# Feature attention stage: one score block copied by ScalarE, k's features clamped by GpSimd and drained by ScalarE

## Chip, cores and metric

One core of one Trainium2 chip. The metric is the device time of one execution in microseconds (us). The engines are PE (TensorE), DVE (VectorE), ACT (ScalarE), POOL (GpSimd) and SP (queue of transfers).

## What is computed

The network has four stages, each followed by a LayerNorm: a linear attention, a mixture of experts, a causal attention with softmax features, and a deep stage of six layers that takes most of the time. The input has 16 sequences of 256 positions and width 128, all in fp32. The change is in the third stage alone:

```python
def _feature_map(t, K):
    f = jnp.einsum('hdf,bhld->bhlf', K, t)
    feats = jnp.concatenate([jax.nn.softmax(f, axis=-1), jax.nn.softmax(-f, axis=-1)], axis=-1)
    return jnp.maximum(feats, EPS)              # EPS = 1e-12
qf = _feature_map(q, Kq); kf = _feature_map(k, Kk)
kv = jnp.cumsum(kf[:, :, :, None, :] * v[..., None], axis=2)
o = jnp.einsum('bhlf,bhldf->bhld', qf, kv)
z = jnp.einsum('bhlf,bhlf->bhl', qf, jnp.cumsum(kf, axis=2)) + EPS
o = o / z[..., None]                            # then heads side by side, @ Wo
```

There are 16 heads of 64. The cumulative sum is computed as causal attention: scores of kf and qf, those above the diagonal set to zero, times v.

## The kernel before

All five engines run programs of their own, ordered by hand and joined by counting semaphores. In the feature stage the unit of the order is the *step*: the function `heads` of each engine loops over h = 0 to 15, one head of sequence n for each step, and puts between the heads the preparation of sequences n+1 and n+2, at steps given by tables of constants. Every engine works its queue strictly in the written order. Sequences 1 to 12 run in a loop that holds two of them; the rest are written out.

**Preparation of a sequence.** It has four *units*: unit 0 is q and unit 1 is k of the first 128 positions, units 2 and 3 are q and k of the second. PE projects in *slots* (L791), each into the one bank `gen`; ACT copies each out (L921, L927) before the next can start. For each unit DVE takes the largest and smallest value of each head (L986, L994), POOL subtracts (L1104, L1107), ACT takes the exponential (L910, 128x2048), DVE sums and takes the reciprocal (L1002, L1004), POOL multiplies (L1116, `scale`) and signals `featured`. PE then turns the unit to feature-major in four slots (L804), in steps 0 to 3 for unit 0, 4 to 7 for unit 1, 8 to 11 for unit 2, 12 to 15 for unit 3. The slots alternate between two banks, `trn`. DVE drains each with a maximum against 1e-12 into `qT` or `kT` (L1012, `keep_features`). Sums and reciprocals stand in steps 13 (the unit 0 of the next sequence), 2, 6 and 10. Projections stand in steps 1 to 13.

**A head.** PE computes three 128x128 blocks of scores into one bank (L817, L818): keys 0 to 127 against all 256 queries, and keys 128 to 255 against queries 128 to 255. The first and third lie on the diagonal; the middle one has all its scores valid. DVE multiplies all three with a table of ones and zeros, `tri` (L1029, `mask`). PE multiplies by V (L829 to L831, `mix`), one step later than the scores. After every second head, in the odd steps, DVE divides by z (L1036, L1039, L1044, `drain_pair`). The outputs are turned (L843), drained by ACT (L939) and multiplied by Wo (L851) in steps 3 and 4; DVE adds them to X (L1051).

Order of PE in step h: scores(h), projection, turning slot h, mix(h-1), then output work. Order of DVE in step h: drain_pair (odd h), maxima, minima or sums where due, mask(h), keep_features of slot h, the addition in step 5. Order of ACT in step h: copy of the projection, exponential (steps 11, 0, 4, 8), drain of the turned output. POOL repeats: subtract unit 0, scale unit 3 of the sequence before, subtract 1, scale 0, copy x, subtract 2, scale 1, subtract 3, scale 2.

Before the first head, PE's slots of sequence 0 and the first of sequence 1 run alone; this is called the lead-in here.

Of the kernel before, what the change touches and what calls it, by code (L numbers as in the profile page):

```python
# [12 lines left out]
ALU = mybir.AluOpType  # L13
# [694 lines left out]
def feature_stage(nc, X, c, weights):  # L708
    with ExitStack() as ctx:
        def sb(name, shape, dt=F32):  # L710
            return ctx.enter_context(nc.sbuf_tensor(name, shape, dt))
# [24 lines left out]
        zr = sb("g_zr", [P, 2, 4])  # L736
        on = sb("g_on", [P, 2, H, HD])
        oT = sb("g_oT", [P, PAIRS, SEQ])
        sco = [psum("g_sco0"), psum("g_sco1")]
        tur = psum("g_tur")  # L740
        wop = tur
# [15 lines left out]
        summed = sem("g_summed")  # L757
        recips = sem("g_recips")
        featured = sem("g_featured")
        scored = sem("g_scored")  # L760
        masked = sem("g_masked")
        mixed = sem("g_mixed")
        z_kept = sem("g_z_kept")
        z_recip = sem("g_z_recip")
# [14 lines left out]
        def _(pe):  # L779
# [15 lines left out]
            def turn_features(n, step, first=False):  # L795
                for slot in [i for i, at_step in enumerate(F_TURN_STEPS) if at_step == step]:
                    unit, a = divmod(slot, 4)

                    if not (first and slot < 2):
                        pe.wait_ge(turn_kept, count(n * F_TURN + slot - 1))  # L800
                    pe.wait_ge(featured, count(n * 4 + unit + 1))
                    for i in range(4):

                        t = pe.transpose(trn[slot % 2][:, i * P:(i + 1) * P],  # L804
                                         ex[:, unit % 2, 4 * a + i].rearrange("p s f -> p (s f)"), c["ident"][:])
                    t.then_inc(turn_full, 1)

            def scores(n, par, h, first):
                N = n * H + h
                if h == 0:  # L810

                    pe.wait_ge(turn_kept, count(n * F_TURN + F_TURN))
                    pe.wait_ge(proj_drained, count(n * F_PROJ + F_PROJ))
                if not (first and h < 2):
                    pe.wait_ge(masked, count(N - 1))
                s = sco[h % 2]
                pe.matmul(s[:, 0:SEQ], kT[:, par, h, 0:P], qT[:, par, h], start=True, stop=True)  # L817
                pe.matmul(s[:, SEQ:SEQ + P], kT[:, par, h, P:SEQ], qT[:, par, h, P:SEQ],  # L818
                          start=True, stop=True).then_inc(scored, 1)

            def mix(n, par, h, first=False):
                N = n * H + h
                pe.wait_ge(masked, count(N + 1))
                if h % 2 == 0 and not (first and h < 4):

                    pe.wait_ge(head_out, count(n * PAIRS + h // 2 - 1))
                a, o = at[:, h % 2], (h % 2) * 130
                bank = acc[h // 2 % 2]
                pe.matmul(bank[:, o:o + 65], a[:, 0:P], V[:, par, 0, h], start=True, stop=True)  # L829
                pe.matmul(bank[:, o + 65:o + 130], a[:, P:SEQ], V[:, par, 0, h], start=True, stop=False)  # L830
                pe.matmul(bank[:, o + 65:o + 130], a[:, SEQ:SEQ + P], V[:, par, 1, h],  # L831
                          start=False, stop=True).then_inc(mixed, 1)
# [68 lines left out]
        @block.scalar  # L901
        def _(act):
            def exps(n, unit, first):

                j = n * 4 + unit
                act.wait_ge(shift_done, count(2 * j + 2))
                if not (first and unit < 2):

                    act.wait_ge(turn_full, count(4 * (j - 1)))
                act.activation(ex[:, unit % 2].rearrange("p h s f -> p (h s f)"),  # L910
                               shifted[:, unit % 2].rearrange("p h s f -> p (h s f)"), ACT.Exp).then_inc(exped, 1)

            def project(n, par, step, first=False):
                for slot in [i for i, at_step in enumerate(F_PROJ_STEPS) if at_step == step]:
                    act.wait_ge(proj_full, count(n * F_PROJ + slot + 1))
                    if slot == 0:
                        t = act.activation(xT[:], gen[:, 0:SEQ], ACT.Copy)
                    else:
                        k, part, a = F_PROJ_ORDER[slot - 1]
                        if part == 2:  # L920
                            t = act.activation(V[:, par, k, 8 * a:8 * a + 8, 0:HD],  # L921
                                               gen[:].rearrange("p (h d) -> p h d", d=HD), ACT.Copy)
                        else:
                            if a == 0 and not first:

                                act.wait_ge(shift_done, count(2 * (n * 4 - 4 + 2 * k + part) + 2))
                            t = act.activation(raw[:, k, part, a * 512:a * 512 + 512], gen[:], ACT.Copy)  # L927
                    t.then_inc(proj_drained, 1)

            def exponentials(n, step, first=False):  # L930
                if step in F_EXP_STEPS:
                    exps(n, F_EXP_STEPS.index(step), first)

            def drain_out(n, q):
                act.wait_ge(o_turned, count(4 * n + q + 1))
                if q == 0:

                    act.wait_ge(projected, count(n))
                act.activation(oT[:, 2 * q:2 * q + 2], tur[:].rearrange("p (r t) -> p r t", t=SEQ),  # L939
                               ACT.Copy).then_inc(oT_ready, 1)  # L940

            def heads(n, par, first=False, ahead=2):
                for h in range(H):
                    if ahead >= 1:
                        project(n + 1, 1 - par, h)
                    if ahead >= 2:
                        project(n + 2, par, h - H)
                    if ahead >= 1:
                        exponentials(n + 1, h)
                    if ahead >= 2:  # L950
                        exponentials(n + 2, h - H)
                    if h in F_OUT_TURN_STEPS:
                        drain_out(n, F_OUT_TURN_STEPS.index(h))
                    if h + H in F_OUT_TURN_STEPS and not first:
                        drain_out(n - 1, F_OUT_TURN_STEPS.index(h + H))

            act.preload_act_table(ACT.Exp)
            act.wait_ge(ready, 1)
            act.wait_ge(ones_set, count(1))
            for step in range(F_FIRST, H):  # L960
                project(0, 0, step, True)
                project(1, 1, step - H)
                exponentials(0, step, True)
                exponentials(1, step - H)
            heads(0, 0, first=True)
            with act.Fori(0, NSEQ // 2 - 2) as i:
                heads(2 * i + 1, 1)
                heads(2 * i + 2, 0)
            heads(NSEQ - 3, 1)
            heads(NSEQ - 2, 0, ahead=1)  # L970
            heads(NSEQ - 1, 1, ahead=0)
            for q, step in enumerate(F_OUT_TURN_STEPS):
                if step >= H:
                    drain_out(NSEQ - 1, q)
# [3 lines left out]
        def _(dve):  # L978
# [27 lines left out]
            def keep_features(n, par, step):  # L1006

                for slot in [i for i, at_step in enumerate(F_TURN_STEPS) if at_step == step]:
                    unit, a = divmod(slot, 4)
                    k, part = divmod(unit, 2)  # L1010
                    dve.wait_ge(turn_full, count(n * F_TURN + slot + 1))
                    dve.tensor_scalar((qT, kT)[part][:, par, 4 * a:4 * a + 4, k * P:(k + 1) * P],  # L1012
                                      trn[slot % 2][:].rearrange("p (h t) -> p h t", t=P), 1e-12, None,
                                      ALU.max).then_inc(turn_kept, 1)

# [8 lines left out]
            def mask(n, h, first):  # L1024
                N = n * H + h
                dve.wait_ge(scored, count(N + 1))
                if not (first and h < 2):
                    dve.wait_ge(mixed, count(N - 1))
                dve.tensor_tensor(at[:, h % 2], sco[h % 2][:, 0:3 * P], tri[:], ALU.mult).then_inc(masked, 1)  # L1029

            def drain_pair(n, r, first=False):
                Q = n * PAIRS + r
# [59 lines left out]
        def _(pool):  # L1092
# [18 lines left out]
            def scale(n, unit):  # L1111
# [1 line left out]
                part = unit % 2  # L1113
                pool.wait_ge(recips, count(j + 1))
                e = ex[:, part]
                pool.tensor_tensor(e, e, er[:, part][:, :, :, None].to_broadcast([P, H, 2, HD]), ALU.mult)\  # L1116
                    .then_inc(featured, 1)

            def stage(n):

# [15 lines left out]
                scale(n, 2)  # L1136

            pool.wait_ge(ready, 1)
            stage(0)
            project(0, first=True)  # L1140
            with pool.Fori(1, NSEQ - 1) as n:
# [1167 lines left out]
```

## Time and profile before

| | |
|---|---|
| median of 3 runs | 4956.29 us (4952.42 to 4957.85) |
| profiled execution, its time | 4950.25 us |
| its span, first to last instruction | 4948.6 us |
| PE busy | 4317.4 us (87%) |
| DVE busy | 3975.7 us (80%) |
| ACT busy | 3045.9 us (62%) |
| POOL busy | 2752.6 us (56%) |
| feature stage | from 493 us to 1284 us of the span |

Busy times are sums over the whole program. The feature stage is about a sixth of the span, and what bounds it has to be read inside it: from the busy times of one sequence, and from what each engine waits for.

### The profile page before, as it was taken

To read this page: it belongs to the slowest core of one execution; us is meant where nothing else is said; L and a number is where in the kernel's file an instruction comes from. 1 tells how busy PE (TensorE), PEld (TensorE's weight loads), DVE (VectorE), ACT (ScalarE), POOL (GpSimd) and SP (SyncE) were. 2 spreads that over 40 slices of the span, in tenths; PEclk is the share of its full clock that TensorE was granted. 3 is DMA by queue.
4 is the path that set the end of the run, shared out by engine and by line. 5 is a ranking of instruction groups with operands and counts; after the bars stand their busy time and mean duration, and the time that the engine had idled before them with its cause. 6 is when DMAs were issued, how large, how long until landed. Compare 5 with 4: busy or idle time off the path is not lost. (4 is left out here: it accounts for less than half of the span.)

```text
span 4948.6 us, 174542 instructions
## 1 busy us (share of the span) xinstructions
PE 4317.4 (87%) x70208; PEld 3409.7 (69%) x70208; DVE 3975.7 (80%) x6281; ACT 3045.9 (62%) x5515; POOL 2752.6 (56%) x1392
## 2 busy tenths in 40 slices
PE   5797899999589899899998998989989989999985
PEld 4565577777467777777777776777777777777774
DVE  5334799998688889888898888988889888998883
ACT  3365333333257777776777777777777767777763
POOL 0222666666266566665666556655666556666561
PEclk9799899999789999999999999999999999999997
DMA  1233000000132233322333224233233232332232
GB/s 48 93 122 119 1 1 0 0 0 1 35 70 58 65 70 82 83 61 57 85 78 74 64 57 99 64 68 71 57 88 77 64 69 66 81 83 60 60 68 55
DMA packets 239161, 303.67 MB, mean 61 GB/s; under 512 B 93940, under 2 KB 129272, under 8 KB 237944
## 3 DMA queue, kind: packets, MB, share of 16 engines
q1 hardware_dynamic: 223192, 247.08, 21.9%
q0 software_dynamic: 15264, 46.14, 2.9%
q8 instruction: 571, 9.36, 0.8%
q14 instruction: 134, 1.10, 0.1%
HBM read 50.37 MB, written 28.84 MB: 16 GB/s over the span
## 5 line engine op out<-in xcount | busy, mean ns | idle before, releaser
L2100 POOL TENSOR_TENSOR raw<-raw,rs 128x1024 f32<-128x1024 f32 x384 | 792.9, 2065 | 1089.7 <-DVE rs L1937 627.8
L2092 POOL TENSOR_TENSOR spare<-raw,table 128x1024 f32<-128x1024 f32 x384 | 914.9, 2393 | 261.7 <-DVE raw L1916 250.8
L1909 DVE TENSOR_TENSOR raw<-raw,table 128x1024 f32<-128x1024 f32 x384 | 732.2, 1907 | 42.4 <-POOL spare L2092 40.4
L1781 ACT ACTIVATE raw<-shared 128x512 f32<-128x512 f32 x768 | 463.5, 603 | 333.9 <-PE shared L1559 310.9
L1557 PE MATMUL shared<-wqkv_lo,xT_hi 128*128 128x512 f32 x1152 | 567.5, 493 | 33.0 <-DVE xT_lo L1946 25.8
L1903 DVE TENSOR_REDUCE ss<-spare 128x16 f32<-128x1024 f32 x384 | 466.1, 1214 | 155.1 <-ACT spare L1786 154.2
L1916 DVE TENSOR_TENSOR raw<-raw,spare 128x1024 f32<-128x1024 f32 x384 | 550.8, 1434 | 13.2
L1612 PE MATMUL trn<-ident,raw 128*128 128x128 f32 x3072 | 484.0, 280 | 13.5 <-POOL raw L2100 4.0
L1558 PE MATMUL shared<-wqkv_hi,xT_lo 128*128 128x512 f32 x1152 | 474.1, 412 | 0.0
L1559 PE MATMUL shared<-wqkv_hi,xT_hi 128*128 128x512 f32 x1152 | 472.2, 410 | 0.0
L1786 ACT ACTIVATE spare<-shared 128x512 f32<-128x512 f32 x768 | 462.3, 602 | 1.9 <-DVE ss L1903 1.9
L1612 PEld LDWEIGHTS trn<-ident,raw 128*128 128x128 f32 x3072 | 351.2, 141 | 142.8 <-issue 49.9
L1665 PE MATMUL acc<-prT,Vw 64*64 64x32 f32 x24576 | 439.0, 221 | 0.1
L1819 ACT ACTIVATE prT<-trn 128x512 f32<-128x512 f32 x384 | 232.2, 605 | 319.6 <-PE trn L1647 317.6
L1665 PEld LDWEIGHTS acc<-prT,Vw 64*64 64x64 f32 x24576 | 396.1, 135 | 23.4 <-issue 0.4
L2115 POOL TENSOR_TENSOR E<-E,rden 128x1024 f32<-128x1024 f32 x192 | 366.4, 1908 | 40.9 <-DVE rden L1982 33.8
L1632 PE MATMUL sco<-kT,qT 64*32 64x64 f32 (+1 forms) x24576 | 378.7, 232 | 11.8 <-issue 11.5
L1647 PE MATMUL trn<-ident,E 128*128 128x128 f32 x1536 | 276.6, 310 | 128.6 <-POOL E L2115 125.8
L1632 PEld LDWEIGHTS sco<-kT,qT 64*32 64x32 f32 x24576 | 255.3, 113 | 187.6 <-issue 183.2
L1681 PE MATMUL shared<-wo,oT 128*128 128x128 f32 x3072 | 376.6, 276 | 2.3 <-ACT oT L1828 1.3
L1681 PEld LDWEIGHTS shared<-wo,oT 128*128 128x128 f32 x3072 | 363.8, 193 | 8.8 <-ACT spare L1786 1.5
L1647 PEld LDWEIGHTS trn<-ident,E 128*128 128x128 f32 x1536 | 214.1, 161 | 192.9 <-issue 148.3
(203 smaller groups left out, 9723.9 us busy)
## 6 DMA issues: line engine op xcount, KB each, us to landing
Vw<-V SPq DMA_DIRECT2D x1344, 128.0 KB
xs<-X SPq DMA_DIRECT2D x144, 128.0 KB, 2.1
Vw<-V SPq DMA_DIRECT2D x192, 64.0 KB
e_plain<-in_L_ffn_W SPq DMA_DIRECT2D x16, 704.0 KB, 4.7
split_hi<-e_high POOLq DMA_DIRECT2D x16, 704.0 KB, 5.9
split_lo<-e_low POOLq DMA_DIRECT2D x16, 704.0 KB, 7.1
wqkv_hi<-split_hi POOLq DMA_DIRECT2D x30, 256.0 KB, 3.1
wqkv_lo<-split_lo POOLq DMA_DIRECT2D x30, 256.0 KB, 3.2
```

What stands on the lines that cost most here:

```text
L1557: pe.matmul(to, a_hi, b_lo, start=True, stop=False)
L1558: pe.matmul(to, a_lo, b_hi, start=False, stop=False)
L1559: return pe.matmul(to, a_hi, b_hi, start=False, stop=True)
L1612: t = pe.transpose(trn[:, r * P:(r + 1) * P], raw[:, par, k, part, at:at + P], c["ident"][:])
L1632: t = pe.matmul(sco[g * WIN:g * WIN + WIN, hp, at:at + back + WIN], qT[lo:lo + 64, r, at_q:at_q + WIN], kT[lo:lo + 64, r, at_q - back:at_q ...
L1647: t = pe.transpose(trn[:, i * P:(i + 1) * P], e[:, 4 * jj + i], c["ident"][:])
L1665: t = pe.matmul(acc[hp][64 * jp:64 * jp + 64, at:at + WIN], Vw[lo:lo + 64, par, k, g, (4 * o + j) * HD:(4 * o + j + 1) * HD], prT[lo:lo + ...
L1681: t = pe.matmul(to[:, k * P:(k + 1) * P], oT[:, r, k * P:(k + 1) * P], wo[:, r], start=(r == 0), stop=(r == PAIRS - 1))
L1909: dve.tensor_tensor(x, x, table[:, part, 0, k][:, None, :].to_broadcast([P, H, HD]), ALU.mult).then_inc(cos_part, 1)
L1916: dve.tensor_tensor(x, x, t2[:, part], ALU.add).then_inc(summed, 1)
L2092: pool.tensor_tensor(dst, src, by[:, None].to_broadcast([P, H, 2, 32]), ALU.mult).then_inc(sin_part, 1)
L2100: pool.tensor_tensor(x, x, rs[:, at:at + H][:, :, None].to_broadcast([P, H, HD]), ALU.mult).then_inc(rotated, 1)
```

## The change

For each head ACT copies the middle block of the scores (`cross`), at the head of its step, and DVE multiplies the two diagonal blocks alone, with one 128x128 table broadcast. ACT's copy waits for DVE's mask of the same head. For the units of k (1 and 3) POOL takes the maximum against 1e-12 itself, after `scale`, with a one-column operation on a tile of its own, `dot`, between the two; `featured` is signalled after the maximum. ACT then copies the turned slots of k out (`keep_k`), at the end of its step, and DVE's `keep_features` does q's slots only. PE waits for both of `masked` and `crossed`, and for `turn_kept` or `k_kept`.

```diff
@@ PE, turn_features
-                        pe.wait_ge(turn_kept, count(n * F_TURN + slot - 1))
+                        last = (slot - 2) % F_TURN
+                        freed = 8 * n - 8 * (slot < 2) + 4 * (last // 8) + last % 4 + 1
+                        pe.wait_ge(k_kept if last // 4 % 2 else turn_kept, count(freed))
@@ PE, scores
-                    pe.wait_ge(turn_kept, count(n * F_TURN + F_TURN))
+                    pe.wait_ge(turn_kept, count(8 * n + 8))
+                    pe.wait_ge(k_kept, count(8 * n + 8))
                     pe.wait_ge(proj_drained, count(n * F_PROJ + F_PROJ))
                 if not (first and h < 2):
                     pe.wait_ge(masked, count(N - 1))
+                    pe.wait_ge(crossed, count(N - 1))
@@ PE, mix
                 pe.wait_ge(masked, count(N + 1))
+                pe.wait_ge(crossed, count(N + 1))
@@ ACT
+            def keep_k(n, par, step):
+                for slot in [i for i, at_step in enumerate(F_TURN_STEPS) if at_step == step]:
+                    unit, a = divmod(slot, 4)
+                    k, part = divmod(unit, 2)
+                    if part == 0:
+                        continue
+                    act.wait_ge(turn_full, count(n * F_TURN + slot + 1))
+                    act.activation(kT[:, par, 4 * a:4 * a + 4, k * P:(k + 1) * P],
+                                   trn[slot % 2][:].rearrange("p (h t) -> p h t", t=P), ACT.Copy).then_inc(k_kept, 1)
+            def cross(n, h, first):
+                N = n * H + h
+                act.wait_ge(masked, count(N + 1))
+                if not (first and h < 2):
+                    act.wait_ge(mixed, count(N - 1))
+                act.activation(at[:, h % 2, P:SEQ], sco[h % 2][:, P:SEQ], ACT.Copy).then_inc(crossed, 1)
@@ ACT, heads
                 for h in range(H):
+                    cross(n, h, first)
                     if ahead >= 1:
                         project(n + 1, 1 - par, h)
...
+                    if ahead >= 1:
+                        keep_k(n + 1, 1 - par, h)
+                    if ahead >= 2:
+                        keep_k(n + 2, par, h - H)
                     if h in F_OUT_TURN_STEPS:
@@ DVE, keep_features
+                    if part == 1:
+                        continue
                     dve.wait_ge(turn_full, count(n * F_TURN + slot + 1))
-                    dve.tensor_scalar((qT, kT)[part][:, par, 4 * a:4 * a + 4, k * P:(k + 1) * P],
+                    dve.tensor_scalar(qT[:, par, 4 * a:4 * a + 4, k * P:(k + 1) * P],
@@ DVE, mask
-                dve.tensor_tensor(at[:, h % 2], sco[h % 2][:, 0:3 * P], tri[:], ALU.mult).then_inc(masked, 1)
+                own, to = (x.rearrange("p (c t) -> p c t", t=P)[:, 0:3:2] for x in (sco[h % 2][:, 0:3 * P], at[:, h % 2]))
+                dve.tensor_tensor(to, own, tri[:, None, 0:P].to_broadcast([P, 2, P]), ALU.mult).then_inc(masked, 1)
@@ POOL, scale
-                pool.tensor_tensor(e, e, er[:, part][:, :, :, None].to_broadcast([P, H, 2, HD]), ALU.mult)\
-                    .then_inc(featured, 1)
+                i = pool.tensor_tensor(e, e, er[:, part][:, :, :, None].to_broadcast([P, H, 2, HD]), ALU.mult)
+                if part == 1:
+                    i.then_inc(scaled, 1)
+                    pool.wait_ge(scaled, count(2 * n + unit // 2 + 1))
+                    pool.tensor_tensor(dot[:], dot[:], dot[:], ALU.mult)
+                    i = pool.tensor_scalar(e, e, 1e-12, None, ALU.max)
+                i.then_inc(featured, 1)
```

The rest of the diff declares `dot` and the three semaphores, sets `dot` to zero once, and calls `keep_k` in the lead-in too.

## Rows read from the trace of the kernel before

**Rows 1.** POOL's timeline: the copies of x of two sequences (start us, duration, instruction).

```profile
837.93 0.40 POOL L1121 COPY g_xs<-X 128x256 f32 x1
...
884.33 0.40 POOL L1121 COPY g_xs<-X 128x256 f32 x1
```

**Rows 2.** Busy time of each engine in 46 us of the steady loop.

```profile
836.00:882.00 46.00, 44.08 (x297) 36.40 (x296) 42.14 (x73) 17.13 (x21) 29.36 (x14) 1.00 0.00 0
```

**Rows 3.** PE's waits, 500 to 1300 us: total us, times, longest.

```profile
PE g_acc L829 <- DVE g_at L1029: 18.1, 15, 1.3
...
PE g_sco L817 <- DVE g_kT L1012: 8.8, 15, 0.8
```

**Rows 4.** Groups of instructions, whole program: busy us, mean ns, idle before.

```profile
L1116 POOL TENSOR_TENSOR g_ex<-g_ex,g_es 128x2048 f32<-128x2048 f32 x64 | 231.8, 3621 | 26.7 <-DVE g_es L1004 26.7
...
L462 POOL COPY e_xs<-X 128x512 f32 x14 | 8.6, 617 | 19.2 <-PE e_xb L512 19.2
...
L1121 POOL COPY g_xs<-X 128x256 f32 x14 | 5.6, 396 | 0.0
```

**Rows 5.** The same view: rows of DVE and ACT.

```profile
L1029 DVE TENSOR_TENSOR g_at<-g_sco,g_tri 128x384 f32<-128x384 f32 x256 | 137.5, 537 | 35.7 <-PE g_sco L818 35.1
...
L1044 DVE TENSOR_TENSOR g_on<-g_acc,g_zr 128x256 f32<-128x256 f32 x128 | 54.3, 424 | 7.1
```

```profile
L604 ACT ACTIVATE e_ggT<-e_tb 128x128 f32<-128x128 f32 x288 | 77.7, 272 | 4.9 <-PE e_ob L562 4.5
```

**Rows 6.** Timeline, steps 1 to 4 of one sequence.

```profile
839.36 0.16 DVE L1036 TENSOR_SCALAR g_zs<-g_acc 128x4 f32<-128x4 f32 x1
...
841.23 0.55 DVE L1029 TENSOR_TENSOR g_at<-g_sco,g_tri 128x384 f32<-128x384 f32 x1
...
843.54 0.60 ACT L921 ACTIVATE g_V<-g_gen 128x512 f32<-128x512 f32 x1 [2.02 <-PE g_gen L791]
...
844.87 0.49 DVE L1029 TENSOR_TENSOR g_at<-g_sco,g_tri 128x384 f32<-128x384 f32 x1
...
845.11 3.62 POOL L1116 TENSOR_TENSOR g_ex<-g_ex,g_es 128x2048 f32<-128x2048 f32 x1
...
845.50 1.02 PE L791 MATMUL g_gen<-g_wf,g_xT 128*128 128x512 f32 x2
...
850.77 0.60 PE L804 MATMUL g_trn<-ident,g_ex 128*128 128x128 f32 x4
```

**Rows 7.** Timeline, steps 10 to 12 of the same sequence.

```profile
869.56 0.49 DVE L1029 TENSOR_TENSOR g_at<-g_sco,g_tri 128x384 f32<-128x384 f32 x1
...
869.81 3.62 POOL L1116 TENSOR_TENSOR g_ex<-g_ex,g_es 128x2048 f32<-128x2048 f32 x1
...
870.19 1.02 PE L791 MATMUL g_gen<-g_wf,g_xT 128*128 128x512 f32 x2
...
873.67 0.60 PE L804 MATMUL g_trn<-ident,g_ex 128*128 128x128 f32 x4
```

**Rows 8.** Timeline, step 12 to the next sequence's step 0.

```profile
874.31 0.69 DVE L1012 TENSOR_SCALAR g_kT<-g_trn 128x512 f32<-128x512 f32 x1 [0.27 <-PE g_trn L804]
...
874.50 0.39 PE L831 MATMUL g_acc<-g_V,g_at 128*128 128x65 f32 x2
...
874.93 0.16 DVE L1036 TENSOR_SCALAR g_zs<-g_acc 128x4 f32<-128x4 f32 x1
...
879.38 0.49 DVE L1029 TENSOR_TENSOR g_at<-g_sco,g_tri 128x384 f32<-128x384 f32 x1
...
879.93 0.44 PE L829 MATMUL g_acc<-g_V,g_at 128*128 128x65 f32 x2 [1.27 <-DVE g_at L1029]
...
882.65 0.68 DVE L1012 TENSOR_SCALAR g_kT<-g_trn 128x512 f32<-128x512 f32 x1
...
883.57 0.67 PE L817 MATMUL g_sco<-g_qT,g_kT 128*128 128x256 f32 x2 [0.56 <-DVE g_kT L1012]
```

**Rows 9.** PE's queue: one of its semaphore waits (ns).

```profile
L826 PEldq EVENT_SEMAPHORE  x54: 51/51/51, 574.6 to 1274.3; - x54
```

More of the change, by code:

```diff
@@ L738, in feature_stage @@
         oT = sb("g_oT", [P, PAIRS, SEQ])
+        dot = sb("g_dot", [P, 1])
         sco = [psum("g_sco0"), psum("g_sco1")]
@@ L759, in feature_stage @@
         featured = sem("g_featured")
+        scaled = sem("g_scaled")
+        k_kept = sem("g_k_kept")
         scored = sem("g_scored")
         masked = sem("g_masked")
+        crossed = sem("g_crossed")
         mixed = sem("g_mixed")
@@ L964, in _ @@
                 exponentials(1, step - H)
+                keep_k(0, 0, step)
             heads(0, 0, first=True)
@@ L1138, in _ @@
             pool.wait_ge(ready, 1)
+            pool.memset(dot[:], 0.0)
             stage(0)
```

## Prediction

> **What bounds the stage now.** I read the page first: the feature stage is a sixth of the span, so I went on inside it. POOL's timeline gives the period: from one copy of x to the next are 46.40 us for each sequence [rows 1]. The busy times of that stretch say what fills it [rows 2]: PE 44.1 of 46 us, DVE 42.1, ACT 17.1, POOL 29.4. PE is the bound and DVE is close behind. PE keeps all its work, so only its idle time can be won. The view of PE's waits has two that come back in each of 15 sequences [rows 3]: a mix that waits for a mask, 18.1 us in all, and the first scores that wait for the last keep of k, 8.8 us. Their sum, 27 us, is about all that relieving DVE can bring. Last I read the timeline of one sequence, to see what each late instruction follows from [rows 6 to 8].
>
> The mix that waits is mix(13), in step 14 [rows 8]. Its mask starts at 879.38, and the work before it on DVE begins at 874.93, with the division that needs mix(11), which ended on PE at 874.50 + 0.39 = 874.89. So that wait is a chain of latencies from PE through DVE (division, minima, sums, mask) and back, not a backlog. The keep of k that stands before the division and that the change takes away ended at 875.00, no later than mix(11) plus 0.1: removing it gives almost nothing there.
>
> The second thing to see is that turning slot 12 is already just in time. POOL scales unit 3 from 869.81 to 873.43, and PE's turning matmul starts at 873.67 [rows 7], 0.24 later. POOL has no slack at this place, though it idles a third of the period.
>
> **The change by its parts, for each sequence.**
>
> *DVE's mask.* 537 ns for 384 columns; the 256-column operation on a PSUM input and a broadcast one takes 424 [rows 5]. So 0.12 less, 16 times: 1.9 us off DVE. *DVE's keeps of k*: 8 of 0.68 [rows 8], 5.4 us off. DVE falls from 42.1 to about 35. Neither is on PE's path except through the chains below.
>
> *ACT.* The copy of 128 columns of PSUM takes 0.27 [rows 5], the keep 0.60 like a projection's copy [rows 6]. 16 x 0.27 + 8 x 0.60 = 9.1 us: ACT goes to 26. Its load is no problem; its order is. The copy `cross` stands at the head of ACT's step and waits for the mask; behind it are queued the copy of the projection, on which PE's next projection waits (one bank), the exponential and the keep of k.
>
> *POOL.* The maximum over 128x2048 does not occur in the trace. Bounds: like the copies, one input read, 396 ns for 256 columns and 617 for 512, thus 0.863 ns a column, 0.396 + 1792 x 0.000863 = 1.94 us; or like the two-input multiply, 3.62 us [rows 4]. It reads one tensor, so I take 1.94. The one-column operation costs the copies' fixed part, 0.396 - 256 x 0.000863 = 0.18, and the wait for the scale's own end some 0.05 (the gap from a mask's end, 879.87, to PE's mix, 879.93 [rows 8]). Together 2.2 us later for `featured`, twice a sequence. POOL goes to 34 us: still not full.
>
> The measured slope of 0.863 ns a column has a rule beside it: the Trainium skill, GPSIMD Engine Reference, section on elementwise cycle accounting, puts a body of up to two operations per element at 1.03 cycles at 1.2 GHz, 0.86 ns, and the trace agrees. The same section gives 1.8 cycles as the best case of a tight loop; by it the maximum would be an estimated 3.1 us, between my two bounds.
>
> *PE.* One more wait in each scores and each mix, 32 a sequence, of 51 ns in its queue [rows 9]. They stand behind matmuls of 0.4 to 1.0 us that are still running, so I take nothing; wholly exposed they would be 1.6 us a sequence, 24 us in all.
>
> **The chains on PE's path.**
>
> *Step 2 to 3.* DVE's chain from the division at 839.36 over mask(1) at 841.23 to mask(2) at 844.87 [rows 6] becomes 0.12 shorter, by the one shorter mask. Mask(2) then ends at 844.75 + 0.37 = 845.12; cross: 845.17 to 845.44; the projection's copy, 0.60: 846.04, and 0.05 to PE: 846.09. PE has wanted the bank at 845.50; ACT had freed it at 843.54 + 0.60 = 844.14. A new stall of 0.6.
>
> *Step 4.* POOL's scale of unit 1, 845.11 + 3.62, + 2.2 + 0.24 = 851.2. PE wants slot 4 at 850.77, now 0.6 later, 851.4 [rows 6]. No stall, by 0.2.
>
> *Step 10 to 12.* Mask(10): 869.44 + 0.37 = 869.81; with cross and copy 870.78, PE had wanted 870.19 [rows 7]: 0.6. But this is swallowed by the next: slot 12 is ready at 873.43 + 2.2 + 0.24 = 875.87 in place of 873.67. POOL's start at 869.81 follows its own subtraction and the minima of step 9, which no part of the change makes earlier. The stall is 2.2.
>
> *Step 13 to 0.* Everything from mix(11) moves by 2.2: mask(13) to 881.58, end 881.95, cross to 882.27, mix(13) at 882.3 instead of 879.93: +2.4. Behind that cross ACT has in its queue the projection's copy, keep, cross(14), keep, cross(15), keep: 4 x 0.60 + 2 x 0.27 = 2.9, ending at 885.2. The first scores follow 0.24 later, at 885.4, where they started at 883.57 [rows 8]: +1.9. The old wait on DVE's last keep (0.56) is so given back in part.
>
> Sum: 0.6 + 1.9 = 2.5 us a sequence. Features are prepared for sequences 1 to 15 inside the heads, 15 times: 37 us. In the lead-in POOL's extra 2.2 us come twice, against DVE queues that are shorter there; I take 0 to 2 us less, 1. By the profiled execution: 4950.3 + 36 = 4986; its time was 6 below the median of the runs, so **4992 us** on the scale of that median.
>
> **Rivals.**
>
> *1. POOL's maximum costs as much as a two-input operation*, 3.62. Then slot 12 comes 1.68 later still, and slot 4 stalls too, by 1.68 - 0.2 = 1.5: 2.5 + 3.2 = 5.7 a sequence, 85 us: **5040**. For it: all of POOL's large operations in this stage cost that. Against: those read two tensors. The rule of 1.8 cycles in the page above lies on this side.
>
> *2. Faster.* If slot 12 is not delayed, DVE's relief can take away both waits of [rows 3], 27 us: **4929**. It needs POOL's clamp to end within the present slack of slot 12, about zero, thus the sums of unit 3 some 2.2 us earlier; it decides from there. For it: DVE loses 7 of 42 us, and sums are its work. Against: the scale starts when POOL's subtraction ends, and the mask of step 13 hangs on mix(11).
>
> *3. No difference.* ACT's held-up copies cost nothing (ACT overlaps them, or the masks come earlier), and relief on DVE removes the wait of mix(13), 1.2 a sequence, and of the first scores, 0.6. Then 2.2 - 1.8 = 0.4, 6 us: **4962**. For it: two waits of DVE do stand on PE's path. Against: the mask of step 13 starts by a chain.
>
> *4. Only POOL's delay counts*, and nothing waits behind ACT's masks and copies: 2.2 at slot 12, less 0.12 for the shorter mask of step 13 and 0.56 for the first scores' wait, which goes [rows 8]: 1.5 a sequence, 23 us: **4979**. For it: ACT is busy a third of the period. Against: its order, above.
>
> **Numbers.** My forecast 0.55, rival 1 0.17, rival 2 0.06, rival 3 0.08, rival 4 0.14. A measurement of this kernel can tell about 0.2%, 10 us, from no change. Faster 0.06, same 0.08, slower 0.86. The likeliest case's own range is 4982 to 5005. The range of 8 in 10 runs from below rival 4 to most of rival 1, with part of PE's exposed waits: 4968 to 5032.
>
> **What would show it.** The period between copies of x: 48.9 instead of 46.4. POOL's maximum: 1.94, right behind a small operation. The matmul of slot 12 waiting for POOL in every sequence, 2 us; the mix of step 14 still waiting, now for ACT's copy; the projection of step 3 waiting 0.5 for ACT. DVE at 35 us and PE at 44 in each period. Wrong would be: a maximum at 3.6; a mask of step 13 that starts much less than 4.4 after mix(11); or PE's queue shown as what its scores and mixes wait for.

## Result and the profile after

The changed kernel takes **5201.83 us** (median of 4 runs, 5199.6 to 5204.28), beside 4957.07 for the kernel before (median of 4): a ratio of 1.0495, 95% interval 1.0477 to 1.0513. The forecast was 4992 with a range of 4968 to 5032: the sign is right, the size is wrong by a factor of seven (245 us more, where 36 were forecast).

I read the profile after in the order of the prediction. POOL's timeline first: the copies of x of two sequences, and what stands between them (start us, duration, instruction).

```profile
855.92 0.40 POOL L1162 COPY g_xs<-X 128x256 f32 x1
...
863.10 3.62 POOL L1152 TENSOR_TENSOR g_ex<-g_ex,g_es 128x2048 f32<-128x2048 f32 x1
866.80 0.19 POOL L1156 TENSOR_TENSOR g_dot<-g_dot 128x1 f32<-128x1 f32 x1
866.95 5.36 POOL L1157 TENSOR_SCALAR g_ex<-g_ex 128x2048 f32<-128x2048 f32 x1
...
914.08 0.40 POOL L1162 COPY g_xs<-X 128x256 f32 x1
```

The period is 914.08 - 855.92 = 58.16 us, against 46.40 in [rows 1]. The maximum takes **5.36 us**; the prediction took 1.94, and its upper bound was the multiply's 3.62, which is unchanged [rows 4]. The small operation ahead of it takes 0.19, as forecast (0.18).

The busy times of that period, then of a part of it without long waits, then of two stretches that stand at PE's two long waits (length, PE, PEld, DVE, ACT, POOL, then the granted clock as a share of full speed; the first row answers to [rows 2]):

```profile
855.92:914.08 58.16, 49.99 (x299) 40.39 (x298) 36.05 (x65) 24.19 (x45) 40.76 (x18) 0.91 0.00 0
856.00:870.00 14.00, 13.34 (x84) 10.42 (x84) 10.52 (x19) 5.72 (x11) 10.86 (x6) 1.00 0.00 0
873.40:876.60 3.20, 3.20 (x17) 3.20 (x17) 1.89 (x4) 0.25 (x1) 0.69 (x1) 0.50 0.00 0
901.00:907.40 6.40, 5.05 (x16) 3.86 (x17) 2.65 (x5) 0.60 (x1) 1.89 (x2) 0.50 0.00 0
```

DVE is at 36.05 as forecast (35) and ACT at 24.19 (26): the work was moved as the change says. POOL is at 40.8, not 34. PE has about as many matmuls as in a period of before (299 and 301), but is busy 50 us with them and not 44.6, and the clock was granted at 0.91, not 1.00. What is new is in the last two rows: PE was granted 0.50, the lower of its two levels, 1.2 GHz in place of 2.4. The first of these stretches goes from about 873.3 to 876.7, 3.4 us, and begins 1 us after the wait ended; the second from about 900.8 to 907.6, 6.8 us, and begins while PE still waits. PE's timeline, steps 4 and 12, shows the waits:

```profile
872.36 0.66 PE L810 MATMUL g_trn<-ident,g_ex 128*128 128x128 f32 x4 [2.89 <-POOL g_ex L1157]
...
873.62 3.48 PE L860 MATMUL g_tur<-g_wo,g_oT 128*128 128x128 f32 x16
876.94 0.60 PE L825 MATMUL g_sco<-g_qT,g_kT 128*128 128x256 f32 x2
...
902.35 1.12 PE L810 MATMUL g_trn<-ident,g_ex 128*128 128x128 f32 x4 [4.51 <-POOL g_ex L1157]
...
904.44 1.16 PE L825 MATMUL g_sco<-g_qT,g_kT 128*128 128x256 f32 x2
...
905.82 1.83 PE L795 MATMUL g_gen<-g_wf,g_xT 128*128 128x512 f32 x2
```

PE waits 2.89 us for the maximum at slot 4 and 4.51 at slot 12. The projection's two matmuls behind the second take 1.83, where they took 1.02 [rows 7]; the 16 of the output product behind the first take 3.48, where they took 2.00:

```profile
847.41 2.00 PE L851 MATMUL g_tur<-g_wo,g_oT 128*128 128x128 f32 x16
```

The groups of 700 to 1300 us, and PE's wait in 560 to 1400 (total, times, longest), which answer to [rows 3 to 5]:

```profile
L1157 POOL TENSOR_SCALAR g_ex<-g_ex 128x2048 f32<-128x2048 f32 x20 | 107.1, 5355 | 0.0
L1065 DVE TENSOR_TENSOR g_at<-g_sco,g_tri 128x256 f32<-128x256 f32 x166 | 66.6, 404 | 47.0 <-PE g_sco L826 46.9
L946 ACT ACTIVATE g_kT<-g_trn 128x512 f32<-128x512 f32 x83 | 49.9, 601 | 56.7 <-PE g_trn L810 56.7
L959 ACT ACTIVATE g_at<-g_sco 128x128 f32<-128x128 f32 x165 | 46.0, 279 | 286.7 <-DVE g_at L1065 286.3
...
PE g_trn L810 <- POOL g_ex L1157: 116.4, 30, 7.7
```

All prices but POOL's came as forecast: the mask 0.40 (0.42), the keep on ACT 0.60, the block's copy 0.28 (0.27).

**A second part that the prediction doesn't have.** The stage ends with the last addition to X. Its row before and its row after:

```profile
1284.08 0.42 DVE L1051 TENSOR_TENSOR X<-X,g_tur 128x256 f32<-128x256 f32 x1 [5.28 <-PE g_tur L851]
```

```profile
1468.28 0.42 DVE L1087 TENSOR_TENSOR X<-X,g_tur 128x256 f32<-128x256 f32 x1 [6.90 <-PE g_tur L860]
```

Up to there the changed kernel has lost 184 us: 11.8 in each of 15 periods, 177, and 7 besides, of which 6 stand in the lead-in (its third copy of x starts at 567.29 in place of 561.35). What follows, the *deep part* from here on, is untouched by the diff, and yet takes 5198.0 - 1468.3 = 3729.7 in place of 4948.6 - 1284.1 = 3664.5: **65 us more**. The view of waits names a line: the score matmuls of the deep stage's loop wait for "issue", that is for nothing that the profile shows. Before, then after:

```profile
PE sco L1632 <- issue: 11.5, 27, 2.2
```

```profile
PE sco L1674 <- issue: 66.9, 31, 3.7
```

PE's timeline at the start of one pass of that loop, before and after:

```profile
2091.05 0.60 PE L1622 MATMUL sco<-mask,identb 128*128 128x512 bf16 x2 [3.57 <-issue]
2091.59 1.04 PE L1632 MATMUL sco<-kT,qT 64*32 64x32 f32 x64
...
2095.30 0.46 PE L1632 MATMUL sco<-kT,qT 64*32 64x64 f32 x12 [0.73 <-issue]
```

```profile
2285.26 0.60 PE L1664 MATMUL sco<-mask,identb 128*128 128x512 bf16 x2 [3.88 <-issue]
2285.79 0.34 PE L1674 MATMUL sco<-kT,qT 64*32 64x32 f32 x17
2289.84 0.96 PE L1674 MATMUL sco<-kT,qT 64*32 64x64 f32 x47 [3.70 <-issue]
```

Both kernels stop for 3.6 to 3.9 us at the loop's first instruction. The second stop comes after 92 matmuls and lasts 0.73 before; after, it comes behind 19 matmuls and lasts 3.70. The same loop, the same instructions, another place in the program.

### The profile page after: what moved, and what is told of

Its sections match the earlier page's. It is cut to its first block and busy times, and to the rows that moved or that the text cites. A ratio compares the mean times of both kernels' runs of the same rounds, so it can differ in the third digit from the quotient of the medians.

```text
span 5198.0 us, 175762 instructions
## 1 busy us (share of the span) xinstructions
PE 4380.4 (84%) x70208; PEld 3456.7 (67%) x70208; DVE 3885.6 (75%) x6153; ACT 3163.1 (61%) x5899; POOL 2929.0 (56%) x1457
## 5 line engine op out<-in xcount | busy, mean ns | idle before, releaser
L1951 DVE TENSOR_TENSOR raw<-raw,table 128x1024 f32<-128x1024 f32 x384 | 746.0, 1943 | 50.2 <-POOL spare L2134 48.3
```

What stands on the lines that cost most here:

```text
L1951: dve.tensor_tensor(x, x, table[:, part, 0, k][:, None, :].to_broadcast([P, H, HD]), ALU.mult).then_inc(cos_part, 1)
```

## The experiments

**Where the code stands: before_pad, after_pad.** Counting PE's instructions in the two programs, the deep loop starts at 6143 before and at 6294 after: the change adds 151, waits for the most part. (A matmul counts as two, its weight load and itself.) In both the second stop lies at instruction 6343 (about 200, and about 49, behind the loop's start). So I moved the loop alone: 151 increments of an unused semaphore on PE ahead of the deep stage of the kernel before, and 49 in the changed kernel.

```diff
+        padded = sem("padded")
...
+            for _ in range(151):
+                pe.sem_inc(padded, 1)
             pe.wait_ge(filled, count(FILLED))
```

> The kernel before, with 151 one-time semaphore increments on PE's queue ahead of the deep stage: it puts PE's code of the deep stage where the changed kernel has it, and changes nothing else. Theory: 65 of the 245 us lie in the deep stage and come from where PE's code stands; PE's second stop behind each loop start (2.3 to 3.7 us where the kernel before shows 0.7) appears here too: 4957 + 65 + 8 for the increments = about 5025 to 5030. Rival: the deep stage is slower for something that the feature stage leaves behind: then 4957 to 4965.

> The changed kernel, with 49 one-time semaphore increments on PE's queue ahead of the deep stage, 200 instructions after the kernel before in place of 151. Theory of the code's place, with pages of 256 instructions: the deep loop starts just at a page's end or start, PE's second stop goes, and the deep stage falls to about 3665 us or less, in all 5202 - 65 = 5137. Rival: no effect, 5202 to 5205.

before_pad: 5024.53 us, ratio 1.0149 (1.0132 to 1.0166) with an unchanged feature stage (period 46.40, last addition at 1284.1). Its deep part is 3746.8 us, 82 longer, of which the increments are 12.6 (PE's idle time ahead of the stage is 45.9 in place of 33.3): 70 from the place alone. after_pad: 5136.69, 65 us less than the changed kernel, deep part 3663.9, as before. The waits of before_pad, then of after_pad:

```profile
PE sco L1633 <- issue: 67.5, 28, 4.0
```

```profile
PE sco L1675 <- issue: 2.4, 5, 1.0
```

That settles the 65 us: the place of the loop makes them, and moving it by 49 instructions takes them back.

**One whole page: before_pad256.** The same edit with 256 increments, to see whether the effect repeats.

> The kernel before with 256 increments on PE's queue ahead of the deep stage. If what counts is the place of the loop's start within pages of 256 instructions, the deep stage is as in the kernel before, though the code stands farther than with 151: about 4951 + 10 to 20 for the increments, and PE's second stop of 2 to 4 us is absent. Rival, that the slowdown grows with the distance or has another period: 5010 or more.

4983.24 us, ratio 1.0055 (1.0036 to 1.0073). The deep part is 3699.2; the increments took 28.7 of that (PE idle 62.0 ahead of it in place of 33.3), so 3670 remain, 6 above the kernel before, though more instructions were added than in before_pad:

```profile
PE sco L1633 <- issue: 11.4, 19, 2.6
```

So the kernel before and this one, 256 instructions apart, behave alike, and those moved by 151 and by 200 behave otherwise. That fits a period of 256 instructions; no further distance was run to show that it repeats. The Trainium skill, Runtime: NRT & Kernel Launch, section on instruction fetch mechanics, states that instructions are fetched in blocks of 256, in order, and that a taken branch to a target outside the present window stops the engine for a fetch. These runs agree with it: the first stop of a pass, at the loop's first instruction, takes 3.6 to 3.9 us. The page does not speak of the second stop; that it is the fetch of the next block, and is the longer the sooner PE gets there (3.70 us behind 19 matmuls, 0.73 behind 92), is inferred from these rows.

**The maximum's price: clamp_as_copy, no_clamp, prices.** In the changed kernel, first the maximum replaced by a copy in place (which reads and writes the same bytes, and leaves the clamp of k out), then both of POOL's new operations removed (k's clamp left out too).

```diff
-                    i = pool.tensor_scalar(e, e, 1e-12, None, ALU.max)
+                    i = pool.tensor_copy(e, e)
```

```diff
-                if part == 1:
-                    i.then_inc(scaled, 1)
-                    pool.wait_ge(scaled, count(2 * n + unit // 2 + 1))
-                    pool.tensor_tensor(dot[:], dot[:], dot[:], ALU.mult)
-                    i = pool.tensor_scalar(e, e, 1e-12, None, ALU.max)
```

> The changed kernel with POOL's maximum over k's features replaced by POOL's copy of the same tile onto itself: k's clamp at 1e-12 is left out. The theory of the chains as predicted, with a price of 1.94 for this operation: the period of a sequence 48.9 us (46.4 before, 58.2 after), the feature stage 791 + 36 = 827 us, and with the 65 us of the deep stage 5058 in all. Rival, that ACT's order costs more than was reckoned: the period stays above 51, over 5090.

> The changed kernel without POOL's maximum and its one-column operation: k's clamp at 1e-12 is left out. If all of the feature stage's loss follows from POOL's operation, the period is 46.4 or less; by the chains, ACT's order alone costs 0.6 to 1.2 a sequence: period 47.0 to 47.6, total 4957 + 65 + 9 to 18 = 5031 to 5040. If DVE's relief pays, the period is 44.5 and the total 4993.

clamp_as_copy: 5048.12 us, ratio 1.0193 (1.0175 to 1.0211). The copy takes 1.89, so this is the kernel that the prediction costed. POOL's timeline:

```profile
904.72 0.40 POOL L1162 COPY g_xs<-X 128x256 f32 x1
...
916.63 1.89 POOL L1157 COPY g_ex<-g_ex 128x2048 f32<-128x2048 f32 x1
...
954.54 0.40 POOL L1162 COPY g_xs<-X 128x256 f32 x1
```

The periods are 48.9, as forecast, and in every second sequence up to 955 us 49.8. The longer ones begin with a stretch at the lower clock, here from 902 to 905.5; in the periods from 954.54 on the clock is at 1.00 and none is longer than 48.9:

```profile
902.20:905.40 3.20, 3.20 (x16) 3.11 (x15) 1.66 (x3) 1.29 (x3) 2.92 (x2) 0.50 0.00 0
```

PE's waits in 560 to 1200:

```profile
PE g_acc L838 <- DVE g_at L1065: 20.1, 13, 1.5
PE g_trn L810 <- POOL g_ex L1157: 14.7, 14, 1.3
```

The first row names DVE, but the timeline of one such wait reads otherwise. The two masks are those of heads 13 and 14, back to back; mix(13) needs the first, which ends near 949.95, and ACT's copy behind it, which ends at 950.27. Mix(13) starts 0.14 after that, so it waits for the copy, as predicted; the profile names head 14's mask, which ends in the same moment.

```profile
949.59 0.69 DVE L1065 TENSOR_TENSOR g_at<-g_sco,g_tri 128x256 f32<-128x256 f32 x2
949.99 0.28 ACT L959 ACTIVATE g_at<-g_sco 128x128 f32<-128x128 f32 x1 [4.88 <-DVE g_at L1065]
...
950.41 0.41 PE L838 MATMUL g_acc<-g_V,g_at 128*128 128x65 f32 x2 [1.55 <-DVE g_at L1065]
```

no_clamp: 5028.77, ratio 1.0155 (1.0138 to 1.0173), a period of 47.68 at a clock of 1.00. Both still pay for the deep loop's place (deep parts 3728.6 and 3729.2), since PE's code is that of the changed kernel. Without POOL's clamp the two moves still cost 47.68 - 46.40 = 1.28 us a sequence: relief on DVE gave nothing that ACT's copies did not take back.

prices puts twelve operations one after the other on POOL in the lead-in of the kernel before, each waiting for the one ahead.

```diff
+            tried = [lambda: pool.memset(a, 1.0), lambda: pool.memset(b, 1.0),
+                     lambda: pool.tensor_copy(o, a),
+                     lambda: pool.tensor_scalar(o, a, 1e-12, None, ALU.max),
...
+                     lambda: pool.tensor_tensor(o, a, b, ALU.add),
+                     lambda: pool.tensor_tensor(o, a, b, ALU.mult)]
+            for k, op in enumerate(tried):
+                op().then_inc(probed, 1)
+                pool.wait_ge(probed, k + 2)
```

> The kernel before, with twelve POOL operations one after the other on unused tiles at the start of the feature stage (their results are not used). If the price of 5.36 us belongs to the form tensor_scalar, then maximum, multiply and add by a constant all cost about 5.36 at 128x2048 and grow with the columns at 2.6 ns each (2.7 us at 1024), whether in place or not. If it belongs to the maximum, multiply and add cost 1.9 to 2.0. If it comes of working in place, the one not in place costs 1.9. The copy of 2048 columns: 1.9; tensor_tensor with two full inputs 3.6.

POOL's timeline of it: a copy, a maximum of 2048 columns, the same in place, a maximum of 1024 and 256 columns, a multiply with a constant, maximum and multiply in one, and a sum of two whole tensors. (A sum with a constant took 5.37.)

```profile
495.51 1.89 POOL L1143 COPY g_shifted<-g_ex 128x2048 f32<-128x2048 f32 x1
497.50 5.38 POOL L1144 TENSOR_SCALAR g_shifted<-g_ex 128x2048 f32<-128x2048 f32 x1
502.95 5.36 POOL L1145 TENSOR_SCALAR g_ex<-g_ex 128x2048 f32<-128x2048 f32 x1
508.39 2.77 POOL L1146 TENSOR_SCALAR g_shifted<-g_ex 128x1024 f32<-128x1024 f32 x1
511.24 0.84 POOL L1147 TENSOR_SCALAR g_shifted<-g_ex 128x256 f32<-128x256 f32 x1
512.17 5.37 POOL L1148 TENSOR_SCALAR g_shifted<-g_ex 128x2048 f32<-128x2048 f32 x1
...
523.08 7.09 POOL L1150 TENSOR_SCALAR g_shifted<-g_ex 128x2048 f32<-128x2048 f32 x1
530.25 4.49 POOL L1151 TENSOR_TENSOR g_shifted<-g_ex 128x2048 f32<-128x2048 f32 x1
```

The price belongs to the form of the instruction, one tensor and a constant, and not to the maximum, to writing in place, or to the reads. The program took 5002.82 us in its single execution; only its rows are used.

**One move at a time: cross_only, keep_on_act.** Of cross_only the edit is the changed kernel's `cross` and halved mask, of keep_on_act the lines below. cross_only keeps ACT's copy of the middle block and leaves k's keeps (with their clamp) on DVE; 46 increments put its deep loop 200 instructions behind that of the kernel before, at the place that it has in after_pad (deep part 3668.6, and no second stop but one of 0.9 us). keep_on_act takes the kernel before and gives ACT k's keeps, with 1e-12 added in place of the maximum; masks stay whole on DVE.

```diff
-                    dve.tensor_scalar((qT, kT)[part][:, par, 4 * a:4 * a + 4, k * P:(k + 1) * P],
+                    dve.tensor_scalar(qT[:, par, 4 * a:4 * a + 4, k * P:(k + 1) * P],
...
+                    act.activation(kT[:, par, 4 * a:4 * a + 4, k * P:(k + 1) * P],
+                                   trn[slot % 2][:].rearrange("p (h t) -> p h t", t=P), ACT.Identity,
+                                   bias=dot[:]).then_inc(k_kept, 1)
```

> Of the change only the copy of the middle block by ACT; k's keeps and their clamp stay on DVE, POOL as before; 46 increments put the deep stage's code clear of the bad place. By the chains, ACT's copy of each projection waits for the mask and then for the cross: stalls of 0.5 to 0.6 in steps 3 and 11, 0.2 in steps 12 and 14: period 47.5 to 48.2, total 4951 + 17 to 27 + 5 for the increments = 4973 to 4983. Rival, that DVE's shorter masks pay for it: period 46.4 or less, 4956 at most.

> Of the change only the move of k's keeps to ACT; ACT adds 1e-12 instead of taking the maximum, POOL and the masks are as before. The first scores' wait for DVE's last keep (0.56 a sequence) goes. By that alone: 15 x 0.56 = 8 us faster, 4943. But POOL's scale of unit 0 is ready for turning slot 0 only at 884.38 in the kernel before, 0.8 after the first scores, and hangs on mix(11) through the minima of step 13 and POOL's subtraction: if this chain sets the period, nothing is gained: period 46.4, 4951.

cross_only: 4980.36 us, ratio 1.0048 (1.0031 to 1.0066), periods of 48.4, and 49.3 in every fourth sequence, where again the clock is at 0.50 for about 3.4 us. PE's timeline shows the price as the prediction described it, a projection that waits for the copy queued behind the block's, and a mix that waits for the block's:

```profile
970.69 1.12 PE L795 MATMUL g_gen<-g_wf,g_xT 128*128 128x512 f32 x2 [0.46 <-ACT g_raw L933]
...
992.41 0.41 PE L835 MATMUL g_acc<-g_V,g_at 128*128 128x65 f32 x2 [1.54 <-ACT g_at L956]
```

keep_on_act: 4944.76, ratio 0.9976 (0.9965 to 0.9987), and a period of 46.40, to the hundredth that of before. DVE is at 37.7 in 46 us and not at 42.1. The wait of the first scores [rows 3] is gone, and turning slot 0, right behind them, waits for POOL instead; PE's waits in 560 to 1200:

```profile
PE g_acc L836 <- DVE g_at L1062: 17.9, 14, 1.3
PE g_trn L810 <- POOL g_ex L1149: 7.2, 14, 0.9
```

So two chains end together at the turn of the period. The second is in the timeline of the kernel before:

```profile
875.67 1.21 DVE L994 TENSOR_REDUCE g_hi<-g_raw 128x16 f32<-128x1024 f32 x1
...
880.76 3.62 POOL L1116 TENSOR_TENSOR g_ex<-g_ex,g_es 128x2048 f32<-128x2048 f32 x1
...
884.44 0.42 PEld L804 LDWEIGHTS g_trn<-ident,g_ex 128*128 128x128 f32 x4 [0.16 <-POOL g_ex L1116]
```

It runs from mix(11) and the division [rows 8] over the minima of step 13 to POOL's subtraction and its scaling of unit 0, which ends at 884.38. Slot 0's weights are loaded 0.06 later, and have waited for it already. The keeps of k don't stand in this chain. The medians differ by 12 us. The profiled execution shows 8 of them at the last addition to X (1276.4 in place of 1284.1), 6 of these in the lead-in (the second interval between copies of x is 35.45 in place of 41.71); none lies in the periods.

**Shortening that chain: reorder, reorder_keep.** If it is the bound, work on it should pay and relief on DVE only then. reorder changes the order alone in the kernel before: unit 0's sums a step earlier, POOL's scale of unit 0 ahead of its shift of unit 1, and the mask of step 13 ahead of its minima. reorder_keep adds keep_on_act to it.

```diff
-F_SUM_STEPS = (-3, 2, 6, 10)
+F_SUM_STEPS = (-4, 2, 6, 10)
...
-                shift(n, 1, first)
                 scale(n, 0)
+                shift(n, 1, first)
...
+                    if h == 13:
+                        mask(n, h, first)
```

> The kernel before with another order around step 13 and nothing moved between engines: sums of unit 0 one step earlier (12 for 13), POOL scales unit 0 ahead of subtracting unit 1, and DVE's mask of head 13 stands before the minima. If the chain mix(11), minima, subtraction, scale of unit 0, slot 0 sets the period, it is cut here by about 3.7 us and the waits of PE at mix(13) and at slot 0 go: period 45.0 to 45.5, 15 x 1 to 1.4 = 15 to 21 us faster, 4930 to 4936. If PE's other waits simply take their place: 46.4, 4951.

> The same order, and k's keeps on ACT, which adds 1e-12 instead of taking the maximum. With POOL's chain out of the way DVE's relief should pay: the first scores no longer wait for DVE's last keep, 0.5 us a sequence better than the reordered kernel alone: period 44.6 to 45.0, 4922 to 4930. If it does not pay, same as the reordered one.

reorder: 4950.88 us, ratio 0.9989 (0.9981 to 0.9998), a period of 46.0 to 46.1 (one of 47.75, with the clock at 0.50 for 3.4 us). That is 0.3 better and not the 1 to 1.4 expected: the mix and slot 0 no longer wait, but the wait of the first scores has grown from 0.6 to 1.2. Then reorder_keep: **4922.85**, ratio 0.9931 (0.9918 to 0.9944), 0.7% faster than the kernel before. The wait of reorder in 560 to 1200, and a period of reorder_keep (columns as above):

```profile
PE g_sco L817 <- DVE g_kT L1012: 15.9, 13, 1.3
```

```profile
910.42:954.80 44.38, 44.38 (x299) 36.83 (x299) 37.93 (x67) 22.08 (x29) 29.75 (x14) 1.00 0.00 0
```

PE is busy in all of it: 2.0 us a sequence, the whole idle time of before, are there to be won, but relief on DVE alone gives 0 and the order alone 0.3. (In this kernel, as in keep_on_act, k gets 1e-12 added and no maximum.)

## Why the prediction was wrong

**The step that failed** is the price of POOL's maximum: "It reads one tensor, so I take 1.94." It takes 5.36, and 3.62, the cost of two inputs, was no upper bound. The trace had copies and two-input operations and not one operation of a tensor with a constant. I bounded it by what it reads. An upper bound from another form of instruction is none, and the range should have said so. The Trainium skill, GPSIMD Engine Reference, section on elementwise cycle accounting, has 1.8 cycles an element as the best case of a tight loop, an estimated 3.1 us for this operation; the measured 5.36 is well above it, and decides. Two terms that the prediction put at nothing failed with it: the clock in the period, and the time of the program behind the stage.

**What the price does,** by the prediction's own chains. Slot 4 would be ready 3.42 later than worked out there, 854.6 against a want of 851.4: a stall of 3.2 (2.89 measured). Slot 12: 2.2 + 3.4 = 5.6, part of it taken up by steps 10 and 11 (4.51 measured). This is a table of distances from the first scores of one head to those of the next, worked out from PE's timelines as medians over five to seven sequences (us):

```
step             2     3     4    10    11    12    13    14    15
before         3.06  4.41  4.41  3.06  2.57  2.62  2.63  3.30  2.97
clamp_as_copy  3.26  4.77  4.41  3.17  3.02  4.03  2.62  3.55  2.73
after          3.26  4.77  9.15  3.18  3.01  8.49  4.03  2.18  2.61
```

Point by point:
- *Step 2 to 3, ACT's order, 0.6:* 0.20 + 0.36 = 0.56 in both. Right.
- *Step 4, no stall by 0.2:* right at the assumed price (4.41), wrong at the true one.
- *Slot 12, 2.2:* 0.11 + 0.45 + 1.41 = 2.0 with the copy. Right.
- *The first scores, 1.9 later:* with the copy, steps 10 to 15 together are 0.11 + 0.45 + 1.41 + 0.25 - 0.24 = 1.98 longer. Right, and so is the sum of 2.5 at the assumed price: the period is 48.9 wherever the clock is at 1.00. The mix of step 14 waits for ACT's copy in clamp_as_copy and in cross_only.
- *PE's added waits, nothing:* nearly right. The view of waits has PE's first scores (L825) waiting for "issue" in the changed kernel, 3.9 us in 12 times in 560 to 1400, where the kernel before has no such row. In clamp_as_copy they start 0.47 behind the end of ACT's last keep (953.83 against 953.36), and 0.24 was reckoned; so some 0.2 of the 1.98 above may be these waits. Their larger effect was elsewhere, below.
- *PE at 44 in each period:* wrong. The clock is at 1.2 GHz for 3.4 us at the one long wait and for 6.8 at the other. From slot 4's matmul to the scores behind it 876.94 - 872.36 = 4.6 go by, in place of 2.9 (850.77 to 853.66 in the kernel before); from slot 12's matmul to the next turning matmul 907.48 - 902.35 = 5.1 in place of 2.6. 1.7 + 2.5 = 4.2 us a sequence.
- *The sum:* 2.5 + 3.2 + 3.4 for the waits + 4.2 for the clock - 1.5, which the last two columns are shorter than with the copy, since the mix of step 14 hardly waits when all is late: 11.8, and 11.8 were measured. This sum was put together after the measurement and partly from it.
- *The rest of the program, nothing:* wrong by 65 us, more than the whole forecast. The prediction counted the added waits by their time and not by the room they take.
- *Rival 2, faster:* the changed kernel doesn't meet its condition (slot 12 in time). keep_on_act meets it, and its gain, 27 us, did not come, because of the chain to slot 0; it takes 4.5 us a period off DVE (38.0 in place of 42.5), and the masks' 1.9 were not taken off with it. The prediction saw that the mix waits by a chain; it did not see that slot 0 is 0.06 from doing so.
- *Rival 1* was the nearest in kind. By its working it gave 5.7 us a sequence; with 5.36 in place of 3.62 it gives 9.1, and the clock and the deep loop are missing from it.

With these put right the sum is 4950.3 + 15 x 11.8 + 65 = 5192; with the 7 us outside the periods, which the prediction had at -1, 5199. The profiled execution took 5199.6. Of the 213 us between it and the forecast for it, 4986, the maximum's price made 15 x 6.6 = 99 by the waits, the clock 63, the deep loop's place 65, the rest 8, less 22 for the shorter last steps.

What stays open is what makes the clock fall. In the changed kernel it falls at both long waits of each sequence (2.9 and 4.5 us). But it also falls in clamp_as_copy, whose longest wait in a period is 1.5 us, behind that wait in every second sequence up to 905 us and then not again before 1280, with the same waits; and no_clamp, with a wait of 1.5 us in each sequence, kept 1.00 from 590 to 1280 us but for 3.4 us in one of them (from 1122.5). So the length of a wait alone doesn't decide it, and no run set that length by itself. What it costs is shown: 1.7 and 2.5 us in the changed kernel, 0.9 in clamp_as_copy (49.8 in place of 48.9).

## What to carry to other kernels

An operation that the trace doesn't hold is priced by the form of its instruction, and when no row has that form, its upper end is open: twelve operations in a lead-in would have said 5.36 where this argument said 1.94. Before work is taken off an engine, follow every chain that ends at the turn of the loop, those with a slack of 0.06 us too; here relief on DVE paid only after the chain beside it was made shorter. And when a part of the program that was not edited becomes slower, look at what its engine waits for behind the start of its loops, and move them by some instructions.

## What the runs showed of the hardware

- POOL, a tensor with a constant, 128 partitions of f32: 5.36 to 5.38 us for 2048 columns, 2.77 for 1024, 0.84 for 256; at 2048 maximum, multiply and sum take the same; 7.09 with two operations in one. A copy takes 1.89, two whole tensors 4.49, and 3.62 if one of them is broadcast. The Trainium skill, GPSIMD Engine Reference, section on elementwise cycle accounting, has 1.03 cycles an element for up to two operations: the copy agrees (0.863 ns a column), the tensor with a constant doesn't, at (5.38 - 2.77) / 1024 = 2.55 ns.
- PE's loop in the deep stage stops at its first instruction for 3.6 to 3.9 us in the passes shown, and a second time by where the loop begins: hardly at all when moved by 200 instructions, 0.7 us a pass in the kernel before, as little when moved by 256, 3.7 to 4.0 when moved by 151. That is 65 to 70 us in this kernel, 1.3%.
- In a loop that otherwise held 1.00, PE was granted 0.50 for 3.4 us at a wait of 2.9 us and for 6.8 at one of 4.5, in every sequence; behind waits of 1.5 us at most it was granted 0.50 for 3.4 us in some sequences and 1.00 in others of the same kernel.
